# DLRM tower: GpSimd's gathers wait for VectorE's low parts of a quad in place of TensorE's transposes

## The reference

```
e = jnp.stack([tbl_0[ids[:, 0]], ..., tbl_26[ids[:, 26]]], axis=1)      # (512, 27, 128)
interactions = einsum('bfd,bgd->bfg', e, e)[:, triu_i, triu_j]          # 351 pairs
h = concatenate([e.reshape(512, -1), interactions, dense_ctx], axis=1)  # (512, 3823)
h = maximum(h @ W_top1 + b_top1, 0)                                     # 512 wide
h = maximum(h @ W_top2 + b_top2, 0)                                     # 256 wide
y = h @ W_top3                                                          # (512, 1)
```

## Time and profile before

| | |
|---|---|
| runs, us | 217.16 median of 3 (215.24 to 219.4) |
| the profiled execution's own time, us | 216.51 |
| its span, first to last instruction, us | 214.7 |
| mean granted TensorE clock | 0.905 |
| TensorE matmul busy | 158.5 us, 74% |
| VectorE, ScalarE, GpSimd busy | 111.5, 102.3, 106.9 us |

### The profile page before, as it was taken

The page is one execution under the profiler, slowest core; times in us unless marked ns, Lnnn a source line. Parts: engine busy times, 40 slices in busy tenths (PEclk is TensorE's granted clock), DMA queues, the critical chain, the costliest instruction groups (busy, mean ns, idle before and its releaser), DMA issues.

```text
span 214.7 us, 2254 instructions
## 1 busy us (share of the span) xinstructions
PE 158.5 (74%) x765; PEld 138.4 (64%) x765; DVE 111.5 (52%) x205; ACT 102.3 (48%) x196; POOL 106.9 (50%) x122
## 2 busy tenths in 40 slices
PE   0139703974796978973999209999999399999895
PEld 0017502863585968863789109898987388989893
DVE  2649505995678827610474158031682750457821
ACT  2658107774559829220496405132584642446501
POOL 5777755774737747774057747374076620002300
PEclk9999975899599999995799757999999769999999
DMA  6999994111211111111002211111012110000000
GB/s 129 362 369 366 350 389 103 49 50 36 53 26 49 49 49 37 53 49 49 0 24 56 52 30 49 37 47 38 3 43 57 37 26 3 0 0 0 0 3 0
DMA packets 9443, 16.75 MB, mean 78 GB/s; under 512 B 3604, under 2 KB 4120, under 8 KB 9304
## 3 DMA queue, kind: packets, MB, share of 16 engines
q1 hardware_dynamic: 5976, 9.53, 13.2%
q0 software_dynamic: 3456, 7.08, 12.3%
HBM read 16.61 MB, written 0.00 MB: 77 GB/s over the span
## 4 chain that ended last, share of the span: by engine, by line
PE 34%; ACT 18%; another core or an unknown queue 17%; DVE 15%; issue 9%; DMA 4%; POOL 1%; ACTq 0%; DVEq 0%
PE h_ps L568 6%; ACT e L273 5%; PE gram_ps L597 5%; PE h_ps L569 5%; PE h_ps L570 5%; DVE e L404 4%; ACT stage_a L301 4%; PE tp_ps L545 3%; DVE stage_a L424 3%; DMA rows<-in_tbl,ids_sb 3%; ACT w_hi L256 2%; ACT y L291 2%; DVE y L416 2%; DVE w_lo L397 2%
## 5 line engine op out<-in xcount | busy, mean ns | idle before, releaser
L241 POOL DMA_INDIRECT rows<-in_tbl,ids_sb x108 | 103.0, 954 | 68.8 <-issue 28.7
L568 PE MATMUL h_ps<-w_hi,e 128*128 128x512 f32 x108 | 54.9, 509 | 14.7 <-DVE e L404 14.7
L404 DVE TENSOR_TENSOR e<-tp_ps,e 128x512 fp32r<-128x512 f32 (+1 forms) x28 | 31.2, 1134 | 40.5 <-ACT e L273 36.3
L273 ACT ACTIVATE e<-tp_ps 128x512 fp32r<-128x512 f32 (+1 forms) x28 | 28.2, 1054 | 44.4 <-PE tp_ps L545 20.8
L569 PE MATMUL h_ps<-w_lo,e 128*128 128x512 f32 x108 | 46.0, 426 | 0.4 <-issue 0.4
L570 PE MATMUL h_ps<-w_hi,e 128*128 128x512 f32 x108 | 45.5, 421 | 1.0 <-issue 1.0
L568 PEld LDWEIGHTS h_ps<-w_hi,e 128*128 128x128 f32 x108 | 33.0, 306 | 18.3 <-DVE e L404 15.7
L545 PE MATMUL tp_ps<-ident,rows 128*128 128x128 f32 x108 | 22.6, 305 | 28.2 <-DVE e L404 13.6
L545 PEld LDWEIGHTS tp_ps<-ident,rows 128*128 128x128 f32 x108 | 14.2, 151 | 33.9 <-DVE e L404 15.1
L570 PEld LDWEIGHTS h_ps<-w_hi,e 128*128 128x128 f32 x108 | 33.2, 307 | 2.4 <-issue 1.1
L569 PEld LDWEIGHTS h_ps<-w_lo,e 128*128 128x128 f32 x108 | 34.0, 314 | 0.5
(11 more groups left out here) (67 smaller groups left out, 127.2 us busy)
## 6 DMA issues: line engine op xcount, KB each, us to landing
stage_a<-in_W_top SPq DMA_DIRECT2D x10, 512.0 KB
w_pairs<-in_W_pairs SPq DMA_DIRECT2D x1, 1792.0 KB
rows<-in_tbl,ids_sb POOLq DMA_INDIRECT x108
y<-in_W_top SPq DMA_DIRECT2D x3, 512.0 KB
w<-in_W_top SPq DMA_DIRECT2D x1, 512.0 KB
y<-in_W_top SPq DMA_DIRECT2D x1, 256.0 KB
out_y<-stage_a SPq DMA_DIRECT2D x4, 0.5 KB
ids_sb<-in_ids SPq DMA_DIRECT2D x1, 40.5 KB, 3.8
```

The lines of the kernel that those rows point to most:

```text
L241: nc.gpsimd.indirect_dma_start(rows[:, n % RING, :], None, tables[f], bass.IndirectOffsetOnAxis(ids_sb[:, t, f:f + 1], 0)).then_inc(rows_l ...
L273: nc.scalar.activation(features(0, fs[0], fs[-1] + 1), tp_ps[k % 2][:, 0:len(fs), :], ACT.Copy).then_inc(e_hi_ready, 1)
L404: nc.vector.tensor_tensor(features(1, fs[0], fs[-1] + 1), tp_ps[k % 2][:, 0:len(fs), :], features(0, fs[0], fs[-1] + 1), ALU.subtract).the ...
L568: nc.tensor.matmul(out, hi, w_hi[:, f, :], start=f == 0, stop=False)
```

## The change

Before it reuses a row of the ring, GpSimd waits for the low parts of the quad to which the old row belonged, in place of that quad's transposes. The count it waits for is the same number on the other semaphore.

```diff
@@ -237,7 +237,7 @@
                     n = t * F + f
                     if n >= RING:
                         old_t, old_f = divmod(n - RING, F)
-                        pool.wait_ge(transposed, old_t * NQ + old_f // QF + 1)
+                        pool.wait_ge(e_lo_ready, old_t * NQ + old_f // QF + 1)
                     nc.gpsimd.indirect_dma_start(
```

## The result

The change makes the kernel slower: 229.41 us median (227.18 to 231.38) against 218.28 for the kernel before on the same chip, ratio 1.058 with a 95% interval of 1.039 to 1.076. The forecast was 218 and its range ended at 226. The profiled execution took 231.38 us with a span of 229.6, against 216.51 and 214.7. Some executions of one kernel are slower than the rest, so a ratio with an interval compares only the fast ones (216.2 and 228.7 us on average here), and the profiled execution of the changed kernel is the slowest of its four.

What follows compares the result with a forecast made beforehand. The prediction took hand-overs between engines as the bound, with about 36 us of signals from an unknown source. 216.5 + 1 (rows) + 2.2 (tile 0) - 4.9 (tile 2) + 2.7 (gram sums) = 217.5, with 0.65 about 218; range 210 to 226.

Steps and rivals of the forecast that it cites:

- New restarts: GpSimd's gathers after a pause: start 0.5 us after the low parts end, at 36.4, 70.5, 115.0 and 161.7.
- Tile 0, +2.2: Train of gathers in tile 0 ends 2.2 us later, and a signal held to its end comes 2.2 later.
- By rows alone the change costs about 1 us: slack is eaten rather than time.: Rows landing later before TensorE's transposes cost about +1 us, left from quad 5 of tile 1; bounds 0 and +2.
- it is no bound over the span of 172 us: GpSimd's gathers take 135 us of its queue in all, so they don't bound the 172 us in which it works.
- Late signals, tile 2: -4.9: Held signals in tile 2 come through, so quad 4 is transposed when its rows are there: -4.9 us, likelier than not.
- Late signals, tile 1: First layer's transposed output in tile 1, signal held 6.71 us: 0 to -6.7 possible, nothing taken.
- Gram sums: +2.7, bounds 0 and 13.4: Gathers pushed into the gram sums of tiles 1 and 2 hold TensorE's signals: +2.7 us in the sum.
- The range: Whole kernel: 210 to 226 us, taking in two rivals at their main values; the forecast's own range was 213.5 to 221.4.
- Rival 2: Tile 1: quad 3's held signal feeds back on the ring, delaying quad 5's transposes by 6.8 us; 225 us, chance 0.27.
- The port rule: Gathers restarting beside VectorE's SBUF-to-SBUF copies can't write descriptors: at most +7.4 us, 225.6 us in all; chance 0.03.

Runs made afterwards that it cites:

- e1: Kernel before, but only the rows of each tile's quad 0 are freed by the low parts, all others by the transposes; 192.09 us, ratio 1.047.
- e6: Changed kernel with 20 more ring rows (34) from tile 1 on, waiting on the low parts; 187.02 us beside 189.66 for the kernel before.
- the repeated pair: Kernel before and changed kernel run again, unaltered, on a chip without held signals; medians 189.66 and 197.10 us, 1.04.
- e7: Changed kernel without the gathers of features 14 to 17 in tiles 1 to 3; 219.55 us, 1.018 of the kernel before.
- e8: Changed kernel without the gathers of features 4 to 7 in tiles 1 to 3; 215.10 us, 0.989 of the kernel before.
- e9: Ring of 34 rows with the kernel before's wait on the transposes; 235.16 us, 1.091 of the kernel before.
- e11: Kernel before with only quad 0 of a tile freed by the low parts, on a chip where the kernel before takes 215.43 us; 226.66 us, 1.058.
- e13: Changed kernel with a ring of 34 rows, waiting on the low parts; 249.03 us against 215.43 for the kernel before, about 1.15.
- e15: Kernel before with a pause behind every eighth gather of tiles 1 to 3; 194.77 us, 1.056.
- e16: Kernel before with a pause behind every fourth gather of tiles 1 to 3; 211.36 us, 1.152.
- e12: Kernel before with quads 1 to 6 freed by the low parts and quad 0 by the transposes; 220.43 us, 1.027.
- e10: Kernel before without any gather of tiles 1 to 3, old ring contents used; 191.99 us in one execution, 0.89.
- e14: Kernel before with each gather of tiles 1 to 3 replaced by a plain SyncE load of the same bytes; 192.34 us, 0.894.

## Why the prediction was wrong, step by step

- **New restarts.** Right in their rule: 36.30 for 36.4. The later ones come at 73.73, 128.00 and 177.03 in place of 70.5, 115.0 and 161.7, as all of the kernel has moved by then. One more stands at 159.17.
- **Tile 0, +2.2.** Right: the piece of unknown source that ends at 53.22 stands for a split that was at 51.24; it begins after the same train, now 2.2 us later, and tile 0's first gram part comes 1.9 us later (58.37 for 56.46).
- **"By rows alone the change costs about 1 us: slack is eaten rather than time."** This is one step that failed, for two reasons. Lateness against transposes of a trace in which signals were held counted that holding as slack. And the gather at 82.48 took 4.09 us where I had counted 1.25. In tile 1 quad 5 is done at 91.03, 7.5 later than the 83.57 of before; 3.2 of that stem from before, so the rows cost 4.3 us in place of 1. TensorE waits for rows of quad 5 2.18, 0.97 and 0.92 us. And on chips without held signals, where a tile takes 38 us, late rows are the loss: e1, e6 and the repeated pair show it, 4 to 6%. And "it is no bound over the span of 172 us" measured GpSimd against a span that the held signals had stretched. In tile 3 the chain runs over the rows as well, from the restart at 177.03 to the last transpose of quad 4 at 185.89, but there they cost only some 0.2 us against the split of quad 0, as forecast.
- **TensorE's clock** had no term in the sum. The waits for rows are followed by twelve products that take 1.5 us longer, and the stall of 8.8 us by a stretch at a granted clock of 0.50. The kernel before has such stretches as well (0.50 from 99.95 to 103.50, behind its stall of 4.89 us), so only what the change adds to the stalls counts.
- **Late signals, tile 2: -4.9.** Right in place and near in size. TensorE was 12.9 later at tile 1's gram parts and is 9.0 later at quads 5 and 6 of tile 2: a gain of 3.9. Quad 4 begins at 134.47, 5.8 later than before, but is split by a wait and ends 7.7 later.
- **Late signals, tile 1: "I take nothing", bounds 0 to -6.7.** Wrong, and outside its bounds: the signal of the first layer's output fell into the later train and was held to its end; TensorE stood 8.82 us in place of 4.89, net +3.9. I had allowed a gain only, as if a train could leave a signal but not catch one.
- **Gram sums: +2.7, bounds 0 and 13.4.** The place was wrong: the gram parts run nearly free (the train before those of tile 1 ends at 112.31; those of tile 2 show one signal 0.9 us late), and the held signals lie at the ends of tiles 1 and 2 (3.9 and 5.1 net). As a size it is the term that was too small.
- **The range.** The forecast's own 213.5 to 221.4 leaves out the upper bound of the gram sums. With it, and with 2 for the rows, the sum ends at 216.5 + 2 + 2.2 - 4.9 + 13.4 + 0.65 = 229.9, so the terms allowed the 229.41 that came, and the range did not.
- **Rival 2** named the right direction, the right kind of mechanism and 225 us, but another signal (quad 3 of tile 1, which was on time). That its number is near is luck.
- **The port rule** was given 0.03. The moves (L424) did nothing to gathers: in no trace does a gather beside them take more than 1.02 us. But the gather at 82.48 lies under the seven subtractions of the pair weights, both of whose inputs are in SBUF:

```profile
81.41 4.34 DVE L437 TENSOR_TENSOR wp<-w_pairs,wp 128x512 fp32r<-128x512 f32 x7
```

It ends 0.8 us behind them. Four more runs have the same: the repeat of the changed kernel (4.11 us at 64.91), e7 (4.24), e8 (4.39) and e9 (4.39). In the kernel before, its repeat, e1 to e6, e11 to e13, e15 and e16 the gathers under these subtractions take at most 1.45 us. The Trainium skill, page "SBUF — State Buffer", section "Who interferes with whom", says that a VectorE instruction with two SBUF inputs contends with a GpSimd instruction that reads SBUF, and not with one that only writes; it adds that a subtraction of this kind was not seen to stall a DMA. The traces agree with the contention for five gathers, and show it absent for all others under the same subtractions, so it isn't known when it strikes; no run here separates the port from what else may delay a gather.

What stays open: on chips of the second kind late rows and held signals both act, and the runs don't split the 5.8% between them. e11 and e12 add up to 8.5%, more than the whole on the result's chip, so the two halves don't seem to be independent. Nor is it shown that the length of a train is what holds a signal. Shown is that signals come late only while gathers of GpSimd run or within 6.0 us of a train's last one (in e9 from 84.24 to 90.22; e10 and e14 have none after tile 0), and that the deep ring, whose gathers pause less, loses most (e9, e13). Why the chips differ is not known either.

## What to carry to other kernels

A wait moved to a later signal costs nothing only if the engine behind it has time to spare, and that is to be read from its work per tile against the tile's length (33.75 of 38 us here), not from the slack in one trace: slack that other stalls have made isn't there when they are absent. Where a producer is near the bound, buy depth rather than an earlier signal, but try it on more than one chip: the ring of 34 rows gave 0.99 on one and 1.15 on another. Add to the price of a new stall the slower products behind it. And a mechanism that can give time back by moving something can take it by the same move; bound it on both sides.

## What the runs showed of the hardware

- While GpSimd issues gathers, and up to 6.0 us behind a train's last one, signals of TensorE reached ScalarE, VectorE and GpSimd late, by up to 15.7 us after the recorded end of the work (e13: 108.70 to 124.44), in the runs of the result and of e7 to e14, where the kernel before takes 215 to 218 us. They weren't seen late on the three chips of the other runs, where it takes 184 to 190 us. No wait of TensorE is put down to an unknown source in any run: ScalarE's and VectorE's signals weren't seen late.
- The same bytes loaded by SyncE hold no signal (192.3 us against 215.4), nor does anything once the gathers are over.
- Five gathers that met a chain of seven VectorE subtractions with both inputs in SBUF took 4.09 to 4.39 us in place of 0.95; under the same chain the gathers of the other runs took 0.94 to 1.45.
- Behind an idle stretch of TensorE of 8.82 us the granted clock was 0.50 from 112.83 to 118.00, and a product of the first layer took 0.63 us in place of 0.40; behind three waits for rows of 2.18, 0.97 and 0.92 us it was 0.62 over 4.48 us.
